# Macaron block with linear attention on 8 cores: a ScalarE step moved, a VectorE step halved, and the output projection reordered

## What is computed

```python
x = x + 0.5 * ffn(layernorm(x), w)           # ffn: x @ sign(w).T
x = x + attn(layernorm(x), Wq, bq, ..., Wo, bo)
x = x + 0.5 * ffn(layernorm(x), w)

# attn, 16 heads of 64, phi(x) = elu(x) + 1
Q, K, V = phi(x @ Wq.T + bq), phi(x @ Wk.T + bk), x @ Wv.T + bv
KV  = einsum('bhnd,bhne->bhde', K, V)        # one 64x64 matrix per head and sequence
out = einsum('bhnd,bhde->bhne', Q, KV) / (einsum('bhnd,bhd->bhn', Q, K.sum(n)) + 1e-6)
return out @ Wo.T + bo
```

## Time and profile before

| what | value |
|---|---|
| median of 2 runs | 2085.96 us (2084.97 to 2086.95) |
| the profiled execution's own time | 2084.22 us |
| its span, slowest core (the one profiled) | 2082.6 us |
| spans of the 8 cores | 2075.3 to 2082.6 us |
| granted TensorE clock, mean of each core | 0.992 to 0.993 |
| PE, ACT, DVE busy | 1767.7 us (85%), 1233.3 us (59%), 759.7 us (36%) |
| DMA | 199.34 MB, mean 96 GB/s |
| the chain that ended last, by engine | PE 54%, ACT 25%, issue 11%, DVE 6%, DMA 3% |

### The profile page before, as it was taken

One profiled execution on the slowest core, in us unless ns is written; L12 is line 12 of the kernel. 1 busy time (PEld: TensorE's weight loads), 2 busy tenths in 40 slices (PEclk: granted clock), 3 DMA queues, 4 the chain that ended last, 5 costly groups with the idle time before them and its releaser, 6 DMA issues.

```text
span 2082.6 us, 33065 instructions; the slowest of 8 cores (2075.3 to 2082.6 us)
## 1 busy us (share of the span) xinstructions
PE 1767.7 (85%) x10784; PEld 793.1 (38%) x10784; DVE 759.7 (36%) x2049; ACT 1233.3 (59%) x2025; POOL 147.5 (7%) x274
## 2 busy tenths in 40 slices
PE   0499899899998998988989989778888888888887
PEld 0233333333333333333333333334444444444443
DVE  2143343333333333333333333134344344443443
ACT  1467767767667767666776676534444444444443
POOL 1000000000000001000000000001101101101010
PEclk9999999999999999999999999999999999999999
DMA  8622222222222223222222222123333333333331
GB/s 181 123 79 77 89 77 79 88 75 81 89 68 88 89 67 119 90 65 88 70 86 89 67 88 69 51 97 125 112 118 120 113 123 119 114 123 117 112 127 76
DMA packets 134630, 199.34 MB, mean 96 GB/s; under 512 B 88384, under 2 KB 88384, under 8 KB 134464
## 3 DMA queue, kind: packets, MB, share of 16 engines
q0 software_dynamic: 32960, 109.08, 15.7%
q1 hardware_dynamic: 101504, 88.15, 14.0%
HBM read 104.87 MB, written 83.89 MB: 91 GB/s over the span
## 4 chain that ended last, share of the span: by engine, by line
PE 54%; ACT 25%; issue 11%; DVE 6%; DMA 3%; ACTq 1%; DVEq 0%; SPq 0%
PE pA L465 34%; PE pA L476 12%; DVE y2t L343 4%; ACT u1b L444 3%; PE pA L470 3%; ACT mnb L399 3%; ACT mxb L401 3%; ACT u2b L450 3%; PE pA L480 2%; ACT nb L359 2%; ACT eb L400 2%; ACT kbQ L387 2%; ACT kbQ L388 2%; DMA y3t<-wfT 2%; PE tpB L455 1%
## 5 line engine op out<-in xcount | busy, mean ns | idle before, releaser
L476 PE MATMUL pA<-wv,u1fm 128*128 128x512 bf16 x1024 | 245.3, 383 | 96.7 <-ACT kbK L403 96.7
L465 PE MATMUL pA<-sw,u2fm 128*128 128x512 bf16 x1024 | 234.6, 383 | 76.7 <-DVE y2t L343 75.5
L476 PE MATMUL pA<-wk,u1fm 128*128 128x512 bf16 x1024 | 242.4, 379 | 18.3 <-ACT kbQ L387 18.3
L444 ACT ACTIVATE u1b<-y2t 128x1024 bf16<-128x1024 f32 x64 | 67.6, 1057 | 299.4 <-DVE y2t L343 299.4
L465 PE MATMUL pA<-wo,attnfm 128*128 128x512 bf16 x1024 | 234.1, 382 | 5.0 <-DVE y3t L323 1.0
L465 PE MATMUL pA<-sw,u0fm 128*128 128x512 bf16 x1024 | 235.6, 384 | 0.0
L465 PE MATMUL pA<-wq,u1fm 128*128 128x512 bf16 x1024 | 232.1, 380 | 0.0
L476 PEld LDWEIGHTS pA<-wv,u1fm 128*128 128x128 bf16 x1024 | 91.0, 98 | 213.2 <-issue 123.8
L384 ACT ACTIVATE u2b<-y1t 128x1024 bf16<-128x1024 f32 x63 | 66.6, 1057 | 176.0 <-DVE y1t L283 175.9
L465 PEld LDWEIGHTS pA<-sw,u2fm 128*128 128x128 bf16 x1024 | 96.4, 98 | 194.8 <-issue 90.8
L314 DVE TENSOR_TENSOR phiQ<-eb,mxb 128x1024 bf16<-128x1024 bf16 x64 | 44.3, 692 | 344.0 <-ACT mxb L401 344.0
(11 more groups left out here) (120 smaller groups left out, 2418.0 us busy)
## 6 DMA issues: line engine op xcount, KB each, us to landing
xt<-x SPq DMA_DIRECT2D x64, 512.0 KB, 3.9
y1scr<-y1t POOLq DMA_DIRECT2D x64, 512.0 KB, 3.8
y1in<-y1scr POOLq DMA_DIRECT2D x64, 512.0 KB, 3.7
out<-y3t SPq DMA_DIRECT2D x64, 512.0 KB, 2.6
qscr<-qfm POOLq DMA_DIRECT2D x64, 256.0 KB, 3.1
qfin<-qscr POOLq DMA_DIRECT2D x64, 256.0 KB, 3.9
qfm<-phiQ SPq DMA_TRANSPOSE x512, 2.3
stg<-wfT SPq DMA_DIRECT2D x4, 512.0 KB, 8.3
```

The lines of the kernel that those rows point to most:

```text
L444: e.activation(u1b[:, 0, :], y2t[:, tw % 2, :], AF.Square, accum_out=sq3b[:, :]).then_inc(sSq3, 1)
L465: mm = e.matmul(dst[:, h*512:(h+1)*512], lhs_fm[:, c*P:(c+1)*P], w_sb[:, c, h*512:(h+1)*512], start=(c == 0), stop=(last and c == 7))
L476: mm = e.matmul(dst[:, h*512:(h+1)*512], lhs_fm[:, c*P:(c+1)*P], w_sb[:, c, h*512:(h+1)*512], start=(c == 0), stop=(last and c == 7))
```

## The change

Three edits.

1. Pass 1, ACT: `mxb` of Q (L401) moves behind the two copies of K out of `pA2` (L403, L404) and behind the wait for them. It still releases DVE's `phiQ`.
2. Pass 2, DVE: `y3t` (L323) is made in two halves of 512 columns, each with its own increment of `vY3`. All other waits for `vY3` are doubled in number.
3. Pass 2, PE: the `wo` projection no longer waits for `y3t` as a whole, and for `attnfm` by halves of the contraction. It waits for both halves of `attnfm` at the start, and takes the `hw` form: each half of the output waits for its half of `y3t`. For the first two tiles there is nothing to wait for in `y3t`, and they keep the other form.

```diff
@@ SP
-                e.wait_ge(vY3, t + 1)
+                e.wait_ge(vY3, 2 * (t + 1))
@@ DVE, pass 2
-                    v.scalar_tensor_tensor(y3t[:, tf % 2, :], pA2[:, :], 0.5, y2t[:, tf % 2, :],
+                    v.scalar_tensor_tensor(y3t[:, tf % 2, 0:512], pA2[:, 0:512], 0.5,
+                                           y2t[:, tf % 2, 0:512],
+                                           ALU.mult, ALU.add).then_inc(vY3, 1)
+                    v.scalar_tensor_tensor(y3t[:, tf % 2, 512:1024], pA2[:, 512:1024], 0.5,
+                                           y2t[:, tf % 2, 512:1024],
                                            ALU.mult, ALU.add).then_inc(vY3, 1)
...
-                        v.wait_ge(vY3, t - 2)
+                        v.wait_ge(vY3, 2 * (t - 2))
@@ ACT, pass 1
                 e.activation(eb[:, :], mnb[:, :], AF.Exp, scale=-1.0)
-                e.activation(mxb[:, :], kbQ[:, :], AF.Relu).then_inc(sEQ, 1)
                 e.wait_ge(tK, t + 1)
                 e.copy(kbK[:, 0:512], pA2[:, 0:512]).then_inc(vKbK, 1)
                 e.copy(kbK[:, 512:1024], pA2[:, 512:1024]).then_inc(vKbK, 1)
                 e.wait_ge(vKbK, 2 * t + 2)
+                e.activation(mxb[:, :], kbQ[:, :], AF.Relu).then_inc(sEQ, 1)
                 e.wait_ge(vPhiQ, t + 1)
@@ PE, pass 2
                     if t > NT:
-                        e.wait_ge(vY3, t - 3)
+                        e.wait_ge(vY3, 2 * (t - 3))
...
                 if 1 <= t <= NT:
-                    if t >= 3:
-                        e.wait_ge(vY3, t - 2)
+                    e.wait_ge(sAttnfm, 2 * t)
                     proj(e, attnfm[:, (t - 1) % 2, :], wo, pA2[:, :], bor, tWo,
-                         cw=(sAttnfm, 2 * t - 1))
+                         hw=(vY3, 2 * t - 5) if t >= 3 else None)
```

## The result

| | median, us | profiled execution, us | its span, us |
|---|---|---|---|
| before, beside it | 2087.33 | 2084.22 | 2082.6 |
| changed | 2113.43 | 2112.25 | 2110.7 |

The changed kernel is slower: the ratio is 1.0128, with a 95% interval of 1.0115 to 1.0142. Forecast were 2112 us and 1.3%. In some executions of every kernel the cores of a die show a lower granted clock and take longer: the medians count these executions, the ratios leave them out. The profiled execution took 28.0 us more than the one before; the sum of the prediction for it was +26.4.

A forecast was written before the change was run, and what follows sets the result against it. ACT was taken to set the pace in pass 1 after the move, a closed loop through `wo` in pass 2. 2084.22 - 4.5 + 30.9 = 2110.6, with the median 1.7 above: 2112 us, range 2094 to 2127.

The forecast's parts named there:

- Pass 1, -4.5 us: Moving `mxb`: 3.7 us gained over tiles 0 to 60, 1.9 over tiles 61 and 62, 1.1 lost in tile 63.
- the round trip ACT, DVE, ACT: Pass 1, first K copy through `mxb` and DVE's `phiQ` to K's `mnb`: 3.07 us, making ACT's later work 0.92 later.
- The gain a tile, 0.08 by the sum and 0.06 by choice: Pass 1, tiles 0 to 60: KV matmuls start 0.08 us earlier, limited by `vb`; 0.06 was taken, 3.7 us in all.
- the +1.1 forecast: Pass 1, tile 63: K's `mnb` follows the first copy by 3.07 instead of 1.20, partly swallowed by 0.81: 1.1 us lost.
- Pass 2, +30.9 us: The `wo` edit adds 0.49 us in each of 62 tiles, 30.4, plus about 0.5 for the first two steps.
- Start +0.29: Pass 2: `wo` waits for all of `attnfm` and starts 0.25 after its end, at 1814.28 instead of 1813.99.
- Form +0.20: Pass 2: `wo` in `wk`'s form takes 4.28 us to the transposes behind it instead of 4.08; bounds 0.18 to 0.22.
- The estimate from the Trainium skill: Pass 2, `wo`'s new form: one exposed weight load costs 0.11 us a tile, putting pass 2 6 us lower.
- A: Rival: ACT is no limit in pass 1, so PE's 0.95 us a tile comes through in full: 2057 us; chance 0.06.
- B: Rival: the loop of pass 2 absorbs the delay of `wo`: 2081 us; chance 0.10.
- C: Rival: the pass 1 hand-over is longer, a shift of 1.25 us, 0.25 over the slack: 2131 us; chance 0.08.
- D: Rival: more idle time in pass 2 lowers PE's clock, slowing `sw`; in every third tile, 2147 us; chance 0.06.
- E: Rival: `wo`'s start costs 0.18 us, signalling as for one semaphore: 2105 us; counted within the forecast's 0.70.

The follow-up runs named there:

- the form without the early wait: Edits 2 and 3 with the second half of `attnfm` awaited only at `wo`'s fifth matmul, pass 1 as before, against the kernel before: 1.0000, 2084.80 us.
- the swapped waits: Changed kernel with `wo`'s first matmul waiting for `y3t`'s half first and `attnfm` second: 2106.71 us, 6.7 under the changed kernel.

## Why the prediction was right

**The sum.** 2112 us was forecast and 2113.43 measured; the runs give each term its own measurement. The sign, the size of pass 2 and the limit in pass 1 were right by the mechanism. That the total came out within 2 us is in part luck: the slowed projections, which the sum left as they were, moved it in both passes.

**Pass 1, -4.5 us.** Measured alone -2.7 (interval -0.8 to -4.8). The mechanism of the usual tile is shown: edit 1 alone leaves a wait for `vb`, and buffers that take ACT's wait for `phiQ` away give the 0.95 a tile back. The term that made it so is the round trip ACT, DVE, ACT: 3.09 against 3.07 forecast. The gain a tile, 0.08 by the sum and 0.06 by choice, was 0.04 to 0.05 in the median tile. It is the small difference of two large numbers; 0.02 of the error is that `mxb` takes 1.06 when it follows a wait and 1.04 when it does not.

The size of the total was met by luck. Of the two tiles that were to gain 0.95 each, one does (18.68 in place of 19.62) and tile 62 gains nothing: ACT's later work comes 0.95 later there too, and the 0.81 that `vb` waited for PE only just covers it, so the KV matmuls start 12.05 behind `wk` where they did 12.02. Tile 63 loses 0.97, near the +1.1 forecast. With the few tiles of 19.85, edit 1 is worth about nothing on a usual core. The slowest core of the kernel before had two slowed `wv` (3.7 us), which were in no term of the sum. In the profiled execution of the whole change the slowed `wq` took 1.6 of that back, and pass 2 began 0.4 us earlier than before.

**Pass 2, +30.9 us.** Measured +29 alone (+28.8 in the traces). The usual tile is what was forecast, 11.63; the trace of before has the slowed `sw` of the earlier trace rows and of 2067.58, that of the changed kernel neither, which accounts for the 2.1 less than forecast. Start +0.29: `wo` follows `attnfm`'s end by 0.25, as taken from rows with two semaphores. Form +0.20: 4.28, as in `wk`. They were not independent of what they replaced, though. The form could have been paid for by the release through `y3t`'s first half (0.23 a tile, of which I saw 0.06 to 0.16). The wait for `attnfm` took exactly that away. The bound of -0.06 for the start was wrong for the reason given at the form without the early wait: it took the end of the transposes for a limit.

**The estimate from the Trainium skill** for the form, 0.11 a tile for one exposed weight load (page "TensorE: Matmul & The Clock Gate", section "LDWEIGHTS (loading the stationary operand)"), is low: the trace of after has 4.28 against 4.08 of before, 0.20.

**The rivals.** A fell with edit 1 alone (0.9987 where it wanted 0.972), and its case was sound in one point: 0.95 of the 1.51 a tile was really to be had, once the shared buffer was gone. B fell with edits 2 and 3 alone: the tile took 11.63. C fell: the shift of ACT's work was 0.95, not 1.25. D came about the other way round: the granted clock is 0.993 in the mean as before, but on the profiled cores pass 2 has two slowed `sw` before and none after, and pass 1 two slowed `wv` before and one slowed `wq` after. Against D the prediction had that no gap grows; the wait for `vb` did, from 1.25 to 2.23, ahead of that `wq`. E, one semaphore's 0.14 where two are waited for, fell with the rows of the changed kernel (0.25) and the swapped waits: the changed kernel lies on the 0.25 side, and the swap moves it by 0.11 a tile.

**Two sums.** The upper bound of pass 1 was 61 x 0.15 - 4.5 = +4.7, not +6. In rival D nine further slowed tiles give 2127.2; it takes ten to pass 2128. Neither moves the forecast.

**Costed at nothing.** `y3t` in halves is hidden in the changed kernel: its second half ends at 1808.96, long before it is needed. In the old place it is not hidden (edit 2 alone, +4 us), which the prediction had as the price if the cover went.

## What to carry to other kernels

A wait that tops the list is worth what the next limit leaves of it: before moving work out of its way, add up the moved instruction's new place with every hand-over behind it, and compare the sum with the slack of the engine that does it. Here the move was right and the single buffer behind it wrong; with a second buffer the same move was worth 61 us in place of 3. Where an instruction waits for several semaphores, wait for the one that comes last last; and an output split in halves gains only when the split result is the last thing waited for.

## What the runs showed of the hardware

- Two waits ahead of one instruction: 0.25 us from the end of the producer to the start when the late one is waited for first, 0.14 when it is waited for last. ACT and DVE as producers with PE waiting show the same two figures. In the kernel before, the order in four places took the tile from 11.15 to 10.90 us, 15.5 us in all. With PE as producer and DVE waiting, `y2t` came 0.15 earlier.
- Tiles of the same kernel differ by a slowed projection: `sw` took 5.30 in place of 3.61 at two places of pass 2 before and at none to two of the variants. It stood behind gaps of 1.39 to 1.84, and other tiles with a gap of the same size ran at full speed (1383.94 in the kernel before: a gap of 1.55, then 3.61).
- In pass 1, the six profiled kernels in which PE waits 1.51 a tile ahead of `wv` have one to three slowed `wv` each (2.73 to 3.54 in place of 1.89), all behind a gap of 1.79 to 1.81; the seven in which it waits 0.57 have none. That is a pattern of these thirteen traces and was not tried by itself. Two such places are 3.7 us, as much as some of the differences above.
- The page puts idle time down only where there is some. In the kernel before, `wo` starts 0.06 us behind the transposes' end (1813.99 against 1813.93), so its release by `y3t` did not show in the groups, and a change of 0.05 to 0.07 in `y3t` did show in the time. The transposes were not the limit that their end makes them seem: with the wait for half of `y3t`, `wo` starts 0.44 behind their start, 0.17 before that end.
